# LoRA merges of the second FFN in two 64-row tiles of TensorE's array instead of products over 96 rows with zeros

## The reference

```python
x = x + attn(cond(x))                 # a routed LoRA layer, then a first FFN block (F = 1248) and power terms
y = x @ W.T + b + LoRA by adapter     # cond2
def lora_linear(v, w, a, b):          # rank 16, SCALING = 2
    return v @ w.T + (v @ a.T) @ b.T * 2
h1 = lora_linear(y, w1, A1, B1)       # 512 -> 1376
h3 = lora_linear(y, w3, A3, B3)       # 512 -> 1376
x = x + lora_linear(silu(h1) * h3, w2, A2, B2)   # 1376 -> 512
```

## Time and profile before

| | |
|---|---|
| time, median of 3 runs | 439.77 us (439.1 to 440.13) |
| the profiled execution's own time | 439.4 us |
| its span, first to last instruction | 437.7 us |
| PE busy | 433.9 us, 99% |
| PEld busy | 357.2 us, 82% |
| DVE busy | 347.3 us, 79% |
| ACT busy | 242.1 us, 55% |
| granted TensorE clock, mean over the span | 1.000 |

### The profile page before, as it was taken

The page is one execution under the profiler, slowest core; times in us unless marked ns, Lnnn a source line. Parts: engine busy times, 40 slices in busy tenths (PEclk is TensorE's granted clock), DMA queues, the critical chain, the costliest instruction groups (busy, mean ns, idle before and its releaser), DMA issues.

```text
span 437.7 us, 5667 instructions
## 1 busy us (share of the span) xinstructions
PE 433.9 (99%) x1969; PEld 357.2 (82%) x1969; DVE 347.3 (79%) x524; ACT 242.1 (55%) x364; POOL 40.6 (9%) x64
## 2 busy tenths in 40 slices
PE   8999999999999999999999999999999999999997
PEld 7788888888888888888888888888888888888886
DVE  4756699676888867987799589799988799988663
ACT  6455443427566446664574658586754566755520
POOL 1003200000000001003400000010001010010000
PEclk9999999999999999999999999999999999999999
DMA  8505800044555655565551024054645444444004
GB/s 276 166 0 155 234 16 1 9 123 104 130 126 130 175 131 128 130 152 144 156 171 49 18 67 97 0 121 98 146 89 137 121 105 107 96 97 100 21 13 180
DMA packets 22171, 47.26 MB, mean 108 GB/s; under 512 B 2880, under 2 KB 4944, under 8 KB 22144
## 3 DMA queue, kind: packets, MB, share of 16 engines
q1 hardware_dynamic: 16992, 32.51, 24.0%
q0 software_dynamic: 5152, 14.39, 17.9%
HBM read 37.98 MB, written 2.10 MB: 92 GB/s over the span
## 4 chain that ended last, share of the span: by engine, by line
PE 99%; DVE 0%; issue 0%; DVEq 0%
PE PS L1589 21%; PE PS L1591 21%; PE PS L1590 21%; PE PS L1435 10%; PE PS L1437 10%; PE PS L1436 10%; PE PS L1705 1%; PE PS L1502 1%; PE PS L1713 0%; PE PS L1455 0%; PE PS L1749 0%; PE PS L1765 0%; PE PS L1766 0%; PE PS L1453 0%; PE PS L1747 0%; PE PS L1722 0%
## 5 line engine op out<-in xcount | busy, mean ns | idle before, releaser
L1589 PE MATMUL PS<-HT,WU 128*128 128x512 f32 x294 | 114.9, 391 | 0.0
L1590 PE MATMUL PS<-HT,WU 128*128 128x512 f32 x294 | 114.5, 390 | 0.0
L1591 PE MATMUL PS<-HT,WU 128*128 128x512 f32 x294 | 114.4, 389 | 0.0
L541 ACT ACTIVATE WU<-raw 128x256 fp32r<-128x256 f32 (+2 forms) x60 | 56.4, 939 | 29.6 <-PE PS L1591 17.0
L911 DVE TENSOR_TENSOR WU<-raw,WU 128x256 fp32r<-128x256 f32 (+2 forms) x61 | 65.0, 1065 | 4.8 <-ACT WU L541 4.7
L541 ACT ACTIVATE PS<-PS 128x512 f32<-128x512 f32 x58 | 33.9, 584 | 61.8 <-PE PS L1591 38.7
L1589 PEld LDWEIGHTS PS<-HT,WU 128*128 128x128 f32 x294 | 55.2, 188 | 12.3 <-DVE PS L1114 1.0
L541 ACT ACTIVATE G<-T 128x512 fp32r<-128x512 f32 (+3 forms) x62 | 49.5, 810 | 28.2 <-DVE T L1152 14.0
L1591 PEld LDWEIGHTS PS<-HT,WU 128*128 128x128 f32 x294 | 55.2, 188 | 11.7
L1590 PEld LDWEIGHTS PS<-HT,WU 128*128 128x128 f32 x294 | 55.2, 188 | 11.0
L911 DVE TENSOR_TENSOR G<-T,G 128x512 fp32r<-128x512 f32 (+3 forms) x59 | 53.2, 914 | 12.3 <-ACT G L541 11.6
(11 more groups left out here) (169 smaller groups left out, 694.5 us busy)
## 6 DMA issues: line engine op xcount, KB each, us to landing
raw<-in_pieces SPq DMA_DIRECT2D x73, 256.0 KB, 3.0
raw<-in_parts SPq DMA_DIRECT2D x14, 512.0 KB, 3.7
raw<-delta POOLq DMA_DIRECT2D x13, 512.0 KB, 5.5
raw<-in_parts POOLq DMA_DIRECT2D x14, 384.0 KB, 5.0
X<-in_x SPq DMA_DIRECT2D x8, 256.0 KB, 5.6
raw<-in_pieces SPq DMA_DIRECT2D x14, 128.0 KB, 2.5
out_x<-X SPq DMA_DIRECT2D x7, 256.0 KB, 2.0
su_raw<-in_stk_up POOLq DMA_DIRECT2D x6, 192.0 KB, 5.8
```

The source lines that it names most:

```text
L541: return nc.scalar.activation(o, i, ACT.Copy)
L1589: pe.matmul(bank, w[:, 1, cols], hi, start=start and kc == 0, stop=False, skip_group_check=not start)
L1590: pe.matmul(bank, w[:, 0, cols], low, start=False, stop=False, skip_group_check=not start)
L1591: mm = pe.matmul(bank, w[:, 0, cols], hi, start=False, stop=kc == 1, skip_group_check=not start)
```

## The change

The 96 rows become two groups of 48, at rows 0 to 47 and 64 to 111, each again high, high, low of 16 rows. A matmul names one group only, and so uses 64 of the array's rows; the other group's matmul stands right behind it and writes the other PSUM bank. A1 and B1 lie in the first group, A3 and B3 in the second, without zeros between them. In an up block, 4 matmuls of 256 columns become 8 of 128 columns, taking turns between the groups. A down block keeps 4 of 256, and the pieces keep one of 512 each, now alternating between groups, since chunks of A2 are laid out over both and B2 stands in both. S2 has three loads instead of four, SU half as many columns. A low part now lies at two places of 16 rows, so VectorE makes it in two operations. The order of PSUM columns of an up block changes, and with it the access patterns of ScalarE's copy to `delta` and of VectorE's merge (two operations of 512 columns instead of one of 1024). On the host the stacks are laid out anew.

```diff
-KS = 96
-LO_A = slice(64, 96)
-LO_B = slice(32, 64)
+
+
+KS = 112
+ROWS = (slice(0, 48), slice(64, 112))
+LO_A = (slice(32, 48), slice(96, 112))
+LO_B = (slice(0, 16), slice(64, 80))
 SU_LOADS = 6
-S2_B = 3 * D
+S2_B = 2 * D
...
-P_TAIL = P_S2 + 4
+P_TAIL = P_S2 + 3
 P_W2 = P_TAIL + 2
-SLOT += [0, 1, 4, 5, 3, 2, 0, 1, 4, 5, 3]
...
         S13 = sb("S13", [KS, D], F32R)
-        S2 = sb("S2", [KS, 4 * D], F32R)
-        SU = sb("SU", [KS, 4 * P], F32R)
-        su_raw = sb("su_raw", [KS, 4 * P])
+        S2 = sb("S2", [KS, 3 * D], F32R)
+        SU = sb("SU", [KS, 2 * P], F32R)
+        su_raw = sb("su_raw", [KS, 2 * P])
...
                 act.wait_ge(merge_done, MERGE["block", q] + 1)
-                nc.scalar.activation(delta[:], PS[:, 6:8, :].rearrange("p b n -> p (b n)"), ACT.Copy,
-                                     scale=SCALING).then_inc(delta_out, 1)
+                if is_up(q):
+                    nc.scalar.activation(delta[:].rearrange("p (k a n) -> p k a n", k=2, a=2),
+                                         PS[:, 6:8, :].rearrange("p a (k n) -> p k a n", k=2), ACT.Copy,
+                                         scale=SCALING).then_inc(delta_out, 1)
+                else:
+                    nc.scalar.activation(delta[:], PS[:, 6:8, :].rearrange("p b n -> p (b n)"), ACT.Copy,
+                                         scale=SCALING).then_inc(delta_out, 1)
...
             def last(q):
                 s2_hi(1)
                 copy_bc(q)
+                copy_e(q)
                 s2_hi(2)
-                copy_e(q)
-                s2_hi(3)
                 tail_hi(0)
                 block_silu(q, 0)
                 tail_hi(1)
@@ -1249,10 +1256,10 @@
 
             def last(q):
                 x_out(q - 1, "c")
-                for k in range(3):
+                for k in range(2):
                     s2_lo(k)
                 add_b(q)
-                s2_lo(3)
+                s2_lo(2)
                 tail_lo(0)
                 add_d(q)
                 tail_lo(1)
...
+            def both_lo(dst, src, places):
+                for rows in places:
+                    last_lo = V.tensor_tensor(dst[rows], src[rows], f32(dst[rows]), ALU.subtract)
+                return last_lo
+
             def s13_lo():
                 dve.wait_ge(hi_w, P_S13 + 1)
-                V.tensor_tensor(S13[LO_A], raw_slot(P_S13)[LO_A], f32(S13[LO_A]), ALU.subtract).then_inc(w_ready, 1)
+                both_lo(S13[:], raw_slot(P_S13), LO_A).then_inc(w_ready, 1)
 
             def s2_lo(k):
                 dve.wait_ge(hi_w, P_S2 + k + 1)
-                rows, cols = LO_A if k < 3 else LO_B, slice(k * D, (k + 1) * D)
-                V.tensor_tensor(S2[rows, cols], raw_slot(P_S2 + k)[rows], f32(S2[rows, cols]), ALU.subtract).then_inc(w_ready, 1)
+                both_lo(S2[:, k * D:(k + 1) * D], raw_slot(P_S2 + k), LO_A if k < 2 else LO_B).then_inc(w_ready, 1)
 
 
             def su_lo(q):
                 dve.wait_ge(hi_su, q + 1)
-                V.tensor_tensor(SU[LO_B], su_raw[LO_B], f32(SU[LO_B]), ALU.subtract).then_inc(su_ready, 1)
+                both_lo(SU[:], su_raw, LO_B).then_inc(su_ready, 1)
 
             def merge_block(q):
                 for p in (P_ONE[q], P_TWO[q]):
                     dve.wait_ge(raw_in[SLOT[p]], raw_count(p))
                 dve.wait_ge(merge_done, MERGE["block", q] + 1)
-                update = PS[:, 6:8, :].rearrange("p b n -> p (b n)")
-                V.scalar_tensor_tensor(merge_region(q), update, SCALING, merge_region(q), ALU.mult, ALU.add).then_inc(merged, 1)
+                for k in range(2):
+                    update = PS[:, 6:8, k * 2 * P:(k + 1) * 2 * P]
+                    own = merge_region(q)[:, k * D:(k + 1) * D].rearrange("p (a n) -> p a n", a=2)
+                    both = V.scalar_tensor_tensor(own, update, SCALING, own, ALU.mult, ALU.add)
+                both.then_inc(merged, 1)
...
             def merge_up(c, odd):
                 pe.wait_ge(su_ready, c // 2 + 1)
                 for d in range(KC):
-                    bank = PB[6 + (1 - d // 2 if odd else d // 2)].rearrange("p (k a n) -> p a k n", k=2, a=2)[:, d % 2]
-                    mm = pe.matmul(bank, S13[:, chunk(d)], SU[:, c % 2 * 2 * P:(c % 2 + 1) * 2 * P], start=True, stop=True)
+                    for tile, rows in enumerate(ROWS):
+                        bank = PB[6 + (1 - tile if odd else tile)][:, chunk((d + 2) % KC if odd else d)]
+                        mm = pe.matmul(bank, S13[rows, chunk(d)], SU[rows, chunk(c % 2)], start=True, stop=True)
                 mm.then_inc(merge_done, 1)
 
             def merge_down(n, odd):
 
                 for j in range(4):
                     bank = PB[6 + (1 - j % 2 if odd else j % 2)].rearrange("p (o j n) -> p j o n", o=2, j=2)[:, j // 2]
-                    o = S2_B + n % 2 * 2 * P
-                    mm = pe.matmul(bank, S2[:, chunk(4 * (n // 2) + j)], S2[:, o:o + 2 * P], start=True, stop=True)
+                    o, rows = S2_B + n % 2 * 2 * P, ROWS[j % 2]
+                    mm = pe.matmul(bank, S2[rows, chunk(2 * (n // 2) + j // 2)], S2[rows, o:o + 2 * P], start=True, stop=True)
                 mm.then_inc(merge_done, 1)
...
             def merge_piece(j):
                 banks_free(("piece", j))
-                pe.matmul(PB[6 + j % 2], S2[:, chunk(TAIL + j)], S2[:, S2_B:S2_B + D], start=True, stop=True).then_inc(merge_done, 1)
+                rows = ROWS[j % 2]
+                pe.matmul(PB[6 + j % 2], S2[rows, chunk((TAIL + j) // 2)], S2[rows, S2_B:S2_B + D],
+                          start=True, stop=True).then_inc(merge_done, 1)
...
-            pe.wait_ge(w_ready, P_S2 + 4)
...
+    def two_tiles(first, second):
+        stack = np.zeros((P,) + first.shape[1:], np.float32)
+        for rows, w in zip(ROWS, (first, second)):
+            stack[rows] = np.concatenate([w] * 3)
+        return stack
+
+    a2 = padded(a["L0_ffn_lora_A2"].T, 4 * D).T.reshape(RANK, 2, KC, 2, P).transpose(1, 3, 0, 2, 4).reshape(2, 2, RANK, D)
+    b2 = a["L0_ffn_lora_B2"].T
+    stacks = [two_tiles(*w) for w in ((a["L0_ffn_lora_A1"], a["L0_ffn_lora_A3"]), a2[0], a2[1], (b2, b2))]
...
+    b1, b3 = (padded(a[key], 2 * SU_LOADS * P).T.reshape(RANK, SU_LOADS, 2 * P).transpose(1, 0, 2)
+              for key in ("L0_ffn_lora_B1", "L0_ffn_lora_B3"))
+    stk_up = np.stack([two_tiles(*w)[:KS] for w in zip(b1, b3)])
```

More of the change, by code:

```diff
@@ L99 @@
 P_S2 = P_S13 + 1
-P_TAIL = P_S2 + 4
+P_TAIL = P_S2 + 3
 P_W2 = P_TAIL + 2
-SLOT += [0, 1, 4, 5, 3, 2, 0, 1, 4, 5, 3]
+SLOT += [0, 1, 4, 5, 2, 0, 1, 4, 5, 3]
 for _q in range(F2, len(BLOCKS)):
@@ L1803, in _ @@
             p4(F2)
-            pe.wait_ge(w_ready, P_S2 + 4)
+            pe.wait_ge(w_ready, P_S2 + 3)
             for q in range(F2 + 1, END + 1):
@@ L1890, in second_ffn @@
         return [piece for q in range(F2, len(BLOCKS)) for piece in block_pieces(up_piece, down, q)] + list(down[TAIL:])
-    a13 = np.concatenate([a["L0_ffn_lora_A1"], a["L0_ffn_lora_A3"]])
-    a2 = padded(a["L0_ffn_lora_A2"].T, C2 * P).T
-    stacks = [np.concatenate([w] * 3) for w in
-              [a13] + [padded(wide(a2[:, k:k + D]), 32) for k in range(0, C2 * P, D)] + [padded(a["L0_ffn_lora_B2"].T, 32)]]
+    def two_tiles(first, second):
[6 more added lines that the diff above has]
+    stacks = [two_tiles(*w) for w in ((a["L0_ffn_lora_A1"], a["L0_ffn_lora_A3"]), a2[0], a2[1], (b2, b2))]
     firsts, tail, parts = first_ffn()
-    pieces += firsts + [padded(w, P) for w in stacks] + tail + list(by_chunk(a["L0_cond2_W"]).transpose(1, 0, 2))
+    pieces += firsts + stacks + tail + list(by_chunk(a["L0_cond2_W"]).transpose(1, 0, 2))
     pieces += second_ffn()
@@ L1900 @@
     assert len(pieces) == PIECES
-    b1, b3 = (padded(a[k], C2 * P).T.reshape(RANK, C2, P) for k in ("L0_ffn_lora_B1", "L0_ffn_lora_B3"))
-    stk_up = np.zeros((SU_LOADS, 2, 2 * RANK, 2, P), np.float32)
-    for c in range(C2):
-        for k, b in enumerate((b1, b3)):
-            stk_up[c // 2, c % 2, k * RANK:(k + 1) * RANK, k if c % 2 == 0 else 1 - k] = b[:, c]
-    stk_up = stk_up.transpose(0, 2, 1, 3, 4).reshape(SU_LOADS, 2 * RANK, 4 * P)
+    b1, b3 = (padded(a[key], 2 * SU_LOADS * P).T.reshape(RANK, SU_LOADS, 2 * P).transpose(1, 0, 2)
+              for key in ("L0_ffn_lora_B1", "L0_ffn_lora_B3"))
+    stk_up = np.stack([two_tiles(*w)[:KS] for w in zip(b1, b3)])
     small = np.concatenate([
@@ L1926 @@
         "lora_b": a["L0_cond2_lora_Bs"],
-        "stk_up": np.concatenate([stk_up] * 3, axis=1),
+        "stk_up": stk_up,
     }
```

## The result

| | before | after |
|---|---|---|
| median of 4 runs | 439.49 us (439.1 to 440.13) | 445.03 us (444.8 to 446.26) |
| span of the profiled execution | 437.7 us | 443.3 us |
| ratio, 95% interval | | 1.0135 (1.0122 to 1.0149) |

A forecast was written before the change was run, and what follows sets the result against it. TensorE was taken as the bound. Up merges +4.4, down +0.85, pieces +0.4, waits given back -0.5 and VectorE +2.36 made +7.5 us on 439.4, or 446.9; 0.37 more to the median gave 447.3, range 443.2 to 453.8.

The forecast's parts named there:

- the sum: All predicted terms on TensorE and VectorE together: +7.5 us over the kernel before.
- What bounds the kernel: TensorE holds 99% of the chain, so start distances count in full; other engines count only where TensorE waits.
- The price of entering: Going from 128-row matmuls into a 64-row group: between nothing and +0.226 us behind a 512-column matmul; upper end taken.
- way in is free: Rival: entering a row tile at the merges costs nothing, only leaving does; +4.1 us, 443.9, chance 0.13.
- no emptying at 64 rows: Rival: merges on 64 rows don't empty the array; 441.3 with pairs (chance 0.10), 447.0 with loads in turns (0.05).
- 0.13 us for running empty: Array emptying between 16-row transposes and 128-row matmuls, read from the old trace, applied to leaving and entering merge groups.
- The middle of a group: Inside a merge, the two row groups' matmuls run in pairs, one 0.12 us spacing per pair; up merge 0.36 us.
- Loads in turns: Rival: weight loads of the two row groups take turns, each merge matmul costing 0.12 us; +13.9, 453.7, chance 0.20.
- faster: Rival: no emptying and half-time loads, merge pairs 0.067 us apart; -1.4 us, 438.4, chance 0.05.
- Given back: 0.5: At three places where p3 waits for add_b, a later TensorE finds the operand ready: -0.5 us.
- VectorE +2.36: Last block of first FFN: three added low-part operations delay add_b, add_d and split activations, all reaching TensorE; +2.36 us.
- From the sum to the median: Step from the profiled execution's 446.9 us to the median of the runs, 0.37 above: 447.3.

The follow-up runs named there:

- e3: Kernel before with its merge matmuls over rows 0 to 63 alone, on one 64-row tile, same number and columns: 444.86 us.
- e6: Changed kernel with merges over all 112 rows of the whole array, up merges kept as eight matmuls of 128 columns: 446.0 us.
- e5: Changed kernel with every merge matmul on the first of the two 64-row tiles: 451.23 us, 6.2 above the changed kernel.
- e4: Changed kernel without tiles, its merge matmuls over all 112 rows at once and 256 columns wide: 442.27 us.
- e2: Kernel before with three more, useless VectorE operations of 16 partitions in the last block of the first FFN: 441.81 us.
- e1: Changed kernel with each low part made by one VectorE operation over all 112 rows instead of two over 16: 443.24 us.
- e10: Kernel before with low parts of S13, S2 and SU made by one VectorE operation over all 96 rows from partition 0: 439.13 us beside 439.52.

## Why the prediction was right, and where its sizes were off

The sign and the range held: 445.03 in 443.2 to 453.8, forecast 447.3. By its own steps, against the ledger without the start (+5.9, where the sum had +7.5):

- **What bounds the kernel.** Right: every distance between starts counted; e3's 6.2 us in the groups arrive as 5.4, and most of the rest is waits that vanish.
- **The price of entering, taken at its upper end (+0.226).** Right in kind. Entering costs as much as leaving; e3 has both, 0.19 each. The rival "way in is free" (443.9) is out, and so is "no emptying at 64 rows". But the prediction's reason for having no row was wrong: it says that a wait for ScalarE covers the way in at the transposes. The trace of the kernel before shows, on TensorE, its loader and ScalarE (which copies what the transposes read):

```profile
16.16 0.39 PE L1437 MATMUL PS<-HT,G 128*128 128x512 f32 x1
16.48 0.67 PE L1468 MATMUL PS<-sm,T 16*128 16x16 f32 x8
```

```profile
16.48 0.57 PEld L1468 LDWEIGHTS PS<-sm,T 16*128 16x128 f32 x8 [0.36 <-issue]
```

```profile
14.76 1.05 ACT L541 ACTIVATE T<-PS 16x512 f32<-16x512 f32 x2
```

ScalarE was done at 15.81, before the last 512-column matmul even started. The first transpose starts 0.320 behind that matmul, as the first merge matmul does after the change (0.318), and the loader's idle time ahead of it is put down to no wait, as at the merges. So the 0.09 of a later start stood in the trace of before, for 16 rows, and the case for "way in is free" was weaker than its 0.13.

- **The term that was mis-sized: 0.13 us for running empty.** It measures 0.10: the first merge start stands 0.318 behind the 512-column one, of which 0.213 is streaming, and on the way out 0.206 less the 0.053 of the columns and less 0.05 that the last merge matmul's own load delays it is again 0.10. That is twice 0.03 for each of the 17 groups, 1.0 us. Why the transposes of the earlier trace rows gave 0.13 is not shown. My estimate: they show 208 ns, while a 128-column matmul with its load ready shows 223 (e6), which is 0.053 of columns and 0.17 of pipeline; 16 columns would then show 0.177, so the last transpose may itself have waited 0.03 for its load, which I counted as emptying. No run tests this.
- **The middle of a group.** Pairs, right; the spacing is 0.110 and not 0.12, since a pair of 128 columns goes at the pace of the load alone: 3 x 0.01 in 11 groups, 0.3 us. Together that is the 1.3 us between the predicted 5.65 for the groups and the measured 4.3. "Loads in turns" is out by the pairs and by e5, and so is "faster": pairs stand 0.110 apart and not 0.067.
- **Given back: 0.5.** The three waits of p3 on add_b are gone (0.16 to 0.17 each), and the three added operations at the start of the second FFN cost nothing, as said; without the longer groups, in e4, they cost 0.16. In all 0.7 came back; the other 0.2 is spread over changes of under 0.08 us, and I have not assigned it.
- **VectorE +2.36.** Measured +2.29, all of it passed on to TensorE: p3 waits 0.70 and p4 1.36 (about 0.7 and 1.4 predicted), and the first tail product 0.19 longer. Its two halves are shown by e2 (the number, 2.1) and e1 (gone with the number, -2.4). The extra 0.11 for a changed start partition was right to take; the low parts of SU and e10 show it from the other side.
- **From the sum to the median.** I added 0.37 for the distance of one execution to the median. The scatter of the start makes that about 0.5 either way, so it was no information. Of the 1.6 us between the sum of 7.5 and the ledger's 5.9, 1.3 are the groups, 0.2 what was given back and 0.1 VectorE.

## What to carry to other kernels

Splitting the array in row tiles pays only for a stretch that is long against its two passages: here each passage cost about 0.19 us, as much as 450 columns of streaming, for groups that hold 0.48 us of work. Where the sum of columns doesn't fall (8 x 128 for 4 x 256), even a free passage would gain next to nothing, since 128 columns are bound by their load: a pair takes 0.110 where one matmul of 256 columns took 0.12. On VectorE count instructions and not partitions; one masked operation over all rows from partition 0 beats two over only the rows that matter, and here even a single one that starts at another partition (e10, by 0.4 us). And ask of a short stretch in the trace whether its neighbours already show the price of the new form: here the transposes on 16 rows did.

## What the hardware showed that I had not expected

- A group of matmuls over 64 rows between matmuls over 128 costs the same on the way in and out: 0.091 and 0.086 us of later starts and 0.10 us of exposed load each (e3). The Trainium skill ("TensorEngine Tiling (Array Packing)", Key Properties) says that a change of mode drains TensorE; the runs agree and put 0.10 us on it, plus 0.10 us of a load that doesn't start early. Matmuls over 112 rows (e4) pay neither.
- The exposed load of the way in is that of the first merge matmul alone (in e3 381 ns against 276 for the others). One passage delays one load, not a series of them.
- Two pieces of 512 columns on two tiles start 4 ns apart, and their group takes 0.855 us, against 1.087 on one tile (e5).
- Three useless VectorE operations on 16 partitions cost 2.1 us of a kernel that is 99% TensorE (e2), since add_b and add_d, for which TensorE waits, are queued behind them.
